# Moving the first batch's value products behind the second scores, into two idle FFN banks

## What is computed

```python
qh, kh, vh = heads(layernorm(x)), heads(ctx), heads(ctx)      # (b, 8, 256, 32)
log_d = lf[..., 1:, None] - lf[..., None, 1:] + i_pre[..., None, :]
d_mat = jnp.exp(where(causal, log_d, -inf) - m)
s_mat = einsum('bhtd,bhsd->bhts', qh, kh) / sqrt(32) * d_mat
denom = maximum(abs(sum(s_mat, -1)), exp(-m)) + 5e-05
h = einsum('bhts,bhsd->bhtd', s_mat, vh) / denom              # then an RMS norm per head and a gain
x = x + h
z = layernorm(x)
a = silu(z @ w1.T * s1) * (z @ w2.T * s2)                     # 256 -> 1024
a = gelu(a @ h1.T * sh1)                                      # 1024 -> 1024
a = gelu(a @ h2.T * sh2)                                      # 1024 -> 1024
x = x + a @ w3.T * s3                                         # 1024 -> 256
```

## Time and profile before

| | us |
|---|---|
| median of 3 runs | 764.7 (764.67 to 765.26) |
| the profiled execution, its own time | 764.41 |
| its span, first to last instruction | 762.7 |
| PE busy | 754.7 (99%) |
| DVE busy | 543.6 (71%) |
| ACT busy | 384.1 (50%) |
| POOL busy | 53.7 (7%) |

### The profile page before, as it was taken

The page is one execution under the profiler, slowest core; times in us unless marked ns, Lnnn a source line. Parts: engine busy times, 40 slices in busy tenths (PEclk is TensorE's granted clock), DMA queues, the critical chain, the costliest instruction groups (busy, mean ns, idle before and its releaser), DMA issues.

```text
span 762.7 us, 15214 instructions
## 1 busy us (share of the span) xinstructions
PE 754.7 (99%) x6296; PEld 631.7 (83%) x6296; DVE 543.6 (71%) x1295; ACT 384.1 (50%) x577; POOL 53.7 (7%) x67
## 2 busy tenths in 40 slices
PE   8999999999999999999999999999999999999998
PEld 4778888888898888988888888888889888898887
DVE  6788786696957868588676877658695784965554
ACT  3566456463365634556454554646335562445332
POOL 3400020000100020000200002000020000000000
PEclk9999999999999999999999999999999999999999
DMA  9393112200022000310005001230102100540640
GB/s 327 98 426 110 35 52 88 108 29 30 29 112 83 29 31 28 140 56 29 31 29 193 0 31 39 87 127 23 37 29 112 55 1 3 172 160 11 177 144 30
DMA packets 14617, 63.46 MB, mean 83 GB/s; under 512 B 2016, under 2 KB 2896, under 8 KB 11728
## 3 DMA queue, kind: packets, MB, share of 16 engines
q1 hardware_dynamic: 12960, 50.12, 18.9%
q0 software_dynamic: 1296, 11.53, 3.9%
q10 hardware_dynamic: 288, 0.79, 0.3%
HBM read 53.94 MB, written 8.50 MB: 82 GB/s over the span
## 4 chain that ended last, share of the span: by engine, by line
PE 94%; DVE 1%; ACT 0%; issue 0%
PE ps_f L1601 31%; PE ps_f L1602 30%; PE ps_f L1566 8%; PE ps_f L1567 8%; PE ps_f L1641 4%; PE ps_f L1642 4%; PE ps_a L1506 2%; PE ps_a L1489 2%; PE ps_a L1341 1%; PE ps_a L1539 1%; PE ps_a L1462 1%; PE ps_a L1455 1%; PE ps_a L1498 0%; PE ps_f L1576 0%; DVE stats L1063 0%; DVE z L1050 0%
## 5 line engine op out<-in xcount | busy, mean ns | idle before, releaser
L1601 PE MATMUL ps_f<-h_hi,wgt 128*128 128x512 f32 x1024 | 401.5, 392 | 0.0
L1602 PE MATMUL ps_f<-h_lo,wgt 128*128 128x512 f32 x1024 | 398.7, 389 | 0.0
L1601 PEld LDWEIGHTS ps_f<-h_hi,wgt 128*128 128x128 f32 x1024 | 192.2, 188 | 40.5
L1602 PEld LDWEIGHTS ps_f<-h_lo,wgt 128*128 128x128 f32 x1024 | 192.3, 188 | 39.0
L752 ACT ACTIVATE work<-ps_f,scl 128x512 f32<-128x512 f32 x128 | 87.5, 684 | 164.9 <-PE ps_f L1602 164.3
L1169 DVE TENSOR_TENSOR h_lo<-work,h_hi 128x512 fp32r<-128x512 f32 x128 | 86.6, 690 | 101.7 <-ACT h_hi L757 100.6
L1566 PE MATMUL ps_f<-h_hi,wgt 128*128 128x512 f32 x252 | 99.1, 393 | 0.0
L1567 PE MATMUL ps_f<-h_lo,wgt 128*128 128x512 f32 x252 | 98.3, 390 | 0.0
L739 ACT ACTIVATE work<-ps_f,scl 128x512 f32<-128x512 f32 x64 | 44.2, 690 | 88.2 <-PE ps_f L1567 87.5
L757 ACT ACTIVATE h_hi<-work 128x512 fp32r<-128x512 f32 x128 | 81.0, 633 | 4.1
L1160 DVE SCALAR_TENSOR_TENSOR work<-ps_f,scl,work 128x512 f32<-128x512 f32 x64 | 48.1, 751 | 39.4 <-PE ps_f L1567 37.9
(11 more groups left out here) (214 smaller groups left out, 685.2 us busy)
## 6 DMA issues: line engine op xcount, KB each, us to landing
decay<-m_rows SPq DMA_DIRECT2D x14, 1024.0 KB, 6.6
decay<-w_cols SPq DMA_DIRECT2D x22, 512.0 KB, 4.2
wgt<-w_cols POOLq DMA_DIRECT2D x5, 1024.0 KB, 11.8
v_aug<-ctx_tok SPq DMA_DIRECT2D x8, 528.0 KB, 3.9
wgt<-w_cols POOLq DMA_DIRECT2D x2, 2048.0 KB, 14.1
x_kept<-xs SPq DMA_DIRECT2D x8, 512.0 KB, 2.6
xs<-x SPq DMA_DIRECT2D x7, 512.0 KB, 3.6
ctxT<-ctx_t SPq DMA_DIRECT2D x7, 512.0 KB, 3.3
```

Of the source, the lines that this page charges most:

```text
L1601: pe.matmul(ps_f[:, bank], w, moving(h_hi[layer][:, k], as_is), start=(k == 0), stop=False)
L1602: last = pe.matmul(ps_f[:, bank], w, moving(h_lo[layer][:, k], as_is), start=False, stop=(k == KH - 1))
```

## The change

The values of b = 0, both tiles, are computed directly behind the scores of b = 1, after group 3, and written into banks turn + 1 and turn + 2 of `ps_f`, those of FFN groups 1 and 2. They wait for the gelus of these groups. Two copies on ACT take them out after gelu 3, and PE waits for those copies after group 4, before group 5 writes bank turn + 1. The stretch after group 5 now holds `make_state`, the values of b = 1 (both tiles, into `ps_a`) and `read_state`; the stretch in the middle of group 7 is gone. `take_near` becomes two calls of two copies each, `take_num` reads SBUF in place of PSUM, and DVE does `take_state` behind the low part of group 4 in place of 5, `take_far` behind 5 in place of 6, `take_num` and `mix_divide` behind 6 in place of 7. The weighted keys lie in the half of `num` that belongs to b = 1.

```diff
-        k_wt = num[:, 0:W * HEADS * DH].rearrange("p (b h d) -> p b h d", b=W, d=DH)
+        def k_wt(j):
+            at = 0 if first(j) else TILES * HEADS * DV
+            return num[:, at:at + W * HEADS * DH].rearrange("p (b h d) -> p b h d", b=W, d=DH)
...
-            return ps_a[:, 2 + b, 0:HEADS * DV]
+            if b == 0:
+                return ps_f[:, (turn_of(j - 1) + 1 + t) % 4, 0:HEADS * DV]
+            return ps_a[:, 2 + t, 0:HEADS * DV]
...
-            def take_near(j):
-                dst = num[:].rearrange("p (b t e) -> p b t e", b=W, t=TILES)[:, :, 0]
-                act.wait_ge(s_pv, Q * j + W)
-                act.activation(dst, ps_a[:, 2:4, 0:HEADS * DV], ACT.Copy).then_inc(s_near, 1)
+            def take_near(j, b):
+                act.wait_ge(s_pv, Q * j + TILES * (b + 1))
+                for t in range(TILES):
+                    last = act.activation(num[:].rearrange("p (b t e) -> p b t e", b=W, t=TILES)[:, b, t], value_out(j, b, t), ACT.Copy)
+                last.then_inc(s_near, 1)
...
                     gelu(i, 0, m)
+                    if a_stage and m == 3:
+                        take_near(j, 0)
                     if a_stage and m == 5:
-                        take_near(j)
+                        take_near(j, 1)
...
-                dve.wait_ge(s_pv, Q * j + Q)
+                dve.wait_ge(s_near, W * j + 1)
                 dst = num[:].rearrange("p (b t e) -> p b t e", b=W, t=TILES)[:, :, 1]
-                dve.tensor_tensor(dst, ps_a[:, 2:4, 0:HEADS * DV], state[:].rearrange("p (b n) -> p b n", b=W), ALU.add)\
+                dve.tensor_tensor(dst, dst, state[:].rearrange("p (b n) -> p b n", b=W), ALU.add)\
                    .then_inc(s_num, 1)
...
             def values(j, t, b):
-                if t == 1:
-
-                    pe.wait_ge(s_near, j + 1)
+                if b == 0:
+                    pe.wait_ge(s_v, 16 * j + 16)
+                    pe.wait_ge(s_gelu, 2 * KH * (j - 1) + 2 + t)
...
                     if a_stage and m == 3:
                         scores(j, 1)
+                        values(j, 0, 0)
+                        values(j, 1, 0)
+                    if a_stage and m == 4:
+                        pe.wait_ge(s_near, W * j)
                     if a_stage and m == 5:
                         make_state(j)
-                        values(j, 0, 0)
                         values(j, 0, 1)
+                        values(j, 1, 1)
+                        read_state(j)
...
-                    if a_stage and m == 7:
-                        read_state(j)
-                        values(j, 1, 0)
-                        values(j, 1, 1)
+                    pass
```

More of the change, by code:

```diff
@@ L530, in weigh_keys @@
                     w = e_cols[:, 0, 1, b * HEADS:(b + 1) * HEADS].rearrange("p (h o) -> p h o", o=1).to_broadcast([P, HEADS, DH])
-                    last = pool.tensor_tensor(k_wt[:, b], v_aug[:, b * TILES, :, 0:DH], w, ALU.mult)
+                    last = pool.tensor_tensor(k_wt(j)[:, b], v_aug[:, b * TILES, :, 0:DH], w, ALU.mult)
                 last.then_inc(s_kwt, 1)
@@ L1099, in mix_divide @@
                 total = heads[:, :, DH]
-                dve.wait_ge(s_near, j + 1)
+                dve.wait_ge(s_near, W * j + 1)
                 dve.wait_ge(s_num, j + 1)
@@ L1245, in batch @@
                         norm_1_stats(g)
+                    if a_stage and m == 4:
+                        take_state(j)
                     if g_stage and m == 4:
@@ L1249, in batch @@
                     if a_stage and m == 5:
-                        take_state(j)
+                        take_far(j)
                     if a_stage and m == 6:
-                        take_far(j)
-                    if a_stage and m == 7:
                         take_num(j)
@@ L1497, in make_state @@
                         strip = slice(h % ROWGRP * DH, (h % ROWGRP + 1) * DH)
-                        last = pe.matmul(ps_a[strip, b, h * DV:(h + 1) * DV], k_wt[:, b, h, :],
+                        last = pe.matmul(ps_a[strip, b, h * DV:(h + 1) * DV], k_wt(j)[:, b, h, :],
                                          v_aug[:, b * TILES, h, :], start=True, stop=True)
```

## The result

The changed kernel takes **778.1 us** (median of 6 runs, 776.48 to 780.14) against 764.68 (6 runs, 764.28 to 765.26) for the kernel before: a ratio of 1.0175 [1.016, 1.0191]. The direction was forecast, the size was not: 13.4 us more in place of 5.6, and outside the range. The profiled execution is the shortest of the six, 776.48 us with a span of 774.4; so the trace accounts for 774.4 - 762.7 = 11.7 us, and what the others have on top must come from the list of runs.

The account below looks back on a forecast made before the run. PE was taken to bound the kernel, never waiting in the rounds. Seven rounds of 0.82 + 0.00 us gave 5.7 us on 764.4, then 0.3 for the median: 770.3 us predicted, own range 769.7 to 772.5, wider range 768.9 to 773.2.

Parts of the forecast that it names:

- No product is added or dropped: PE's stream: same products, one stretch of small products fewer per round, giving back 0.10 us.
- The two cancel: 0.00 us for a round: PE per round: 0.10 us from the saved stretch against 0.11 more for `read_state`; bounds 0.10 either way.
- The waits for gelu: PE before the two value tiles of b = 0: waits of 0.21 and 0.61 us, 0.82 lost per round.
- 0.00 for the stretch saved and the new neighbour: PE per round: one small-product stretch fewer and `read_state` following small products net to 0.00 us.
- the 0.11 of the forecast: `read_state` after small products: weight load no longer hidden, 1.10 us as in the head instead of 0.99.
- its own bound of 0.10 less: Lower bound on the 0.00 us per round: `read_state`'s weight load is hidden after all.
- No wait before L1547, and none at group 5: PE at `read_state` and group 5: no waiting, with 0.25 and 1.7 us to spare.
- Nothing that moves on DVE is on the path: DVE's moved work, including the norm 3 us later, was claimed not to delay PE.
- The clock falls (1%): Rival, 1%: PE's gelu waits drop the clock to 1.2 GHz, group 4 takes twice as long; 796 us.

Follow-up runs that it names:

- stride4: Changed kernel with four heads of the first value tile in two 64-row strips, one repeated wait dropped, 11 tiny products in the head; 769.75 us, 1.0061.
- b20: Kernel before the change with 5 tiny extra products (20 instructions) in the head; 767.65 us, 1.0038.
- sh64: Changed kernel with 16 tiny extra products (64 instructions) in the head; 779.04 us, one run.
- later: Changed kernel with scores of b = 1 and values of b = 0 behind group 4 instead of 3, values in the next two banks; 774.51 us, 1.0120.
- ctx_late: Changed kernel with the load of the next context waiting for the end of the values of b = 1; 774.99 us, 1.0123.
- sh128: Changed kernel with 32 tiny extra products (128 instructions) in the head; 777.61 us, one run.
- strips64: Changed kernel with all value products of pairs 1 to 7 in two strips of 64 rows instead of four of 32; 778.29 us, 1.0174.

## Why the prediction was wrong

**The step that failed** is the one that begins "No product is added or dropped". From it the sum priced the new order by the products and the waits for other engines, "The two cancel: 0.00 us for a round", and multiplied by seven. That PE's own stream has to be fetched, and that a stretch which uses 256 instructions in 1.3 us can outrun the fetch, was put at nothing: it had no term and no rival. The sum was also a price per round, and this cost is none: it falls on single rounds by the count of all instructions ahead. In the traced run it is 5.3 us; stride4, without it, takes 769.75, and b20 has it alone, 2.7 us for one. (The forecast number has a slip of its own: 770.1 and 0.3 are 770.4.)

**The waits for gelu** were right in place, number and nearly in size: 0.24 and 0.48 idle against 0.21 and 0.61. Gelu 2 ends 2.51 us after the scores' start, as before. From the scores' start to group 4 it is 3.34 us (3.2 forecast, 1.10 + 1.26 before), so 0.98 for 0.82: PE starts 0.14 after the end of the gelu (447.11 + 0.67 to 447.92), not 0.05, at both waits.

**"0.00 for the stretch saved and the new neighbour"** was mis-sized by -0.17. The saved stretch gives back 0.115 us: the 80 FFN products of the round and their changes take 18.53 us in place of 18.65. And `read_state` takes 0.92 us against the 0.99 of the earlier trace rows, not 1.10. The first weight load of it, before (pair 5), in the head before, and in the changed kernel (pair 5):

```profile
454.85 1.09 PEld L1539 LDWEIGHTS ps_a<-state,zT 128*128 128x128 f32 x8
...
29.97 0.97 PEld L1539 LDWEIGHTS ps_a<-state,work 128*128 128x128 f32 x8
...
458.91 0.97 PEld L1547 LDWEIGHTS ps_a<-state,zT 128*128 128x128 f32 x8
```

Before, it starts 0.22 us ahead of the first product (455.07), under an FFN product. In the head and in all seven rounds of the changed kernel it starts together with that product (458.91), and the second product record follows the first by 0.217 us in place of 0.112. So the load is not hidden behind the small products, and the 0.11 of the forecast was paid: the row of the head was the right one for this. By the pull-ahead rule of the Trainium skill (TensorE: Matmul & The Clock Gate, "What happens when you issue a matmul"), as the prediction applied it, the load would have been hidden; these rows do not agree. What the head's 1.10 also held is the neighbour behind: from the last record of `read_state` to the next product it is 0.21 us where values follow (head and before), 0.03 where FFN products do. That is 0.18 less, and the sum had nothing for it. The term lies outside its own bound of 0.10 less. (The parts as read here make 0.18 or 0.19; the -0.17 is what the whole round leaves.) Together 0.98 - 0.17 = 0.81, and seven times that is 5.7: two errors of size that cancel on the bare sum, which is luck.

**"No wait before L1547, and none at group 5"**: right; DVE had been idle for 1.90 us when `take_state` was released. **"Nothing that moves on DVE is on the path"**: the regular rounds bear it out.

**"The clock falls (1%)"**: behind the 14 gelu waits of 0.24 and 0.48 us in the traced run it did not, as argued. But it falls to 0.50 at a stop or just behind it in four other traces, for 3.4 or 6.8 us: at PE's idle time of 3.0 us in sh64 (pair 2), 2.1 in later (pair 7), 1.9 in ctx_late (pair 4) and 1.5 in sh128 (pair 7). It stays full at 2.4 and 2.0 in the changed kernel, 2.2 in b20 and 2.1 in later (pair 1), so the length of the stop alone does not decide. The rival looked at the wrong gaps. In the traced run of the changed kernel the mean clock is 1.000; in the other five runs it is 0.993 to 0.997, and a mean that is 0.3% lower stands for some 2 us of work lost in 774. That fits the 1.6 us by which the median exceeds the traced run, but those executions left no trace, so it is argued and not shown.

**What stays open.** Each stop's length: 0.3 to 3.2 us start to start at distances within the band, with `ctxT`'s load a part of it in pairs 3 and 4. It goes with the moment at which the packet starts: at the stops in the loops that is from 0.1 us before (sh128, pair 4) to 3.2 us after (sh64, pair 2) PE's crossing one block earlier, and what sets it is not shown. The lead of some 40 instructions, and the moment of the request, are inferred from the packets' starts. Why the remainder is 193 and not 0 isn't known either; my count begins at the first instruction that I can see.

## What to carry to other kernels

## What the runs showed of the hardware that was not expected

PE stops for its instructions for 0.3 us (sh64, pair 1) to 3.2 us (sh64, pair 2), start to start less the usual pace, and goes on 2.3 to 2.4 us after the packet's start in the changed kernel; 20 instructions in the head move the time of a 765 us kernel by 2.7 us. At a stop of 1.5 to 3.0 us the granted clock can fall to 0.50 (for 6.8 us in sh64, 173.1 to 179.9), so one costs up to 5.9 us; at waits of 0.5 us it didn't. Weights of 128 columns are not loaded ahead behind value products with 32 columns (458.91 in the changed kernel), while behind an FFN product they are (454.85 before). A value product with 64 columns of weights takes 62 ns (the x64 of B in strips64, 458.68 to 460.67, 1.99/32; 72 ns in A, 2.29/32), one with 32 columns 20 ns (1.26/64): the wider strip costs three times the narrow one.
